# Gated delta stage: state update ahead of norm and key products' turn, first state products in other banks, dense copy of the block decay

## The reference, cut to what matters

```
def step(S, inp):                      # per head, S is 64 x 64
    qt, kt, vt, at, bt = inp
    err = jnp.einsum('bhij,bhj->bhi', S, kt) - vt
    S = at[..., None] * S - bt[..., None, None] * (err[..., None] * kt[:, :, None, :])
    o = jnp.einsum('bhij,bhj->bhi', S, qt)
    return (S, o)
...
o = (o - mu) / jnp.sqrt(var + EPS) * ln_w + ln_b
g = jax.nn.sigmoid(x @ Wg.T).reshape(Bb, Tt, H, DV)
o = (o * g).reshape(Bb, Tt, H * DV)
return o @ Wo.T
```

## Time and profile before

| | us |
|---|---|
| median of 3 runs | 3102.03 (3100.22 to 3104.4) |
| the profiled execution's own time | 3108.88 |
| its span | 3107.1 |
| PE busy | 2466.5 (79%) |
| PEld busy | 1716.8 (55%) |
| DVE busy | 2238.8 (72%) |
| ACT busy | 1270.0 (41%) |
| POOL busy | 272.3 (9%) |
| mean granted clock of TensorE | 0.860 of full speed |

### The profile page before, as it was taken

How to read it: one execution, slowest core, us unless ns; L and a number is a source line. 1 busy time by engine, 2 the same in 40 slices (tenths; PEclk the granted TensorE clock), 3 DMA queues, 4 the chain that set the end, 5 groups by cost and what they waited for, 6 DMA issues and landing times. The chain is left out here.

```text
span 3107.1 us, 64860 instructions
## 1 busy us (share of the span) xinstructions
PE 2466.5 (79%) x25297; PEld 1716.8 (55%) x25349; DVE 2238.8 (72%) x4089; ACT 1270.0 (41%) x2846; POOL 272.3 (9%) x281
## 2 busy tenths in 40 slices
PE   6877788887777777878956999999767756778776
PEld 5777777776777777763323666666322221222375
DVE  6999999999999999971033777777256656665555
ACT  3333333333333333323224777776411132556333
POOL 0000000000000000000031010100022311110342
PEclk9788878788888778879987999999978877999788
DMA  4111101111111101102018999995000001110521
GB/s 170 29 30 30 30 21 24 29 30 29 30 29 30 30 17 28 29 4 62 0 34 226 240 231 247 231 240 135 34 0 0 0 33 50 41 41 17 156 68 57
DMA packets 204444, 214.39 MB, mean 69 GB/s; under 512 B 31126, under 2 KB 190246, under 8 KB 198790
## 3 DMA queue, kind: packets, MB, share of 16 engines
q1 hardware_dynamic: 201769, 205.37, 25.5%
q0 software_dynamic: 2400, 4.94, 0.5%
HBM read 135.30 MB, written 74.70 MB: 68 GB/s over the span
## 5 line engine op out<-in xcount | busy, mean ns | idle before, releaser
L1284 DVE TENSOR_REDUCE ra_top<-ps 128x1 f32<-128x512 f32 x256 | 161.5, 684 | 96.5 <-PE ps L1088 90.7
L2552 DVE TENSOR_REDUCE dl_ZO<-dl_XP 128x64 f32<-128x128 f32 (+6 forms) x448 | 219.6, 490 | 15.4
L2226 PE MATMUL ps<-dl_kqN,dl_ST 64*64 64x32 f32 x4096 | 201.2, 274 | 18.2 <-DVE dl_ST L2575 18.2
L2226 PEld LDWEIGHTS ps<-dl_kqN,dl_ST 64*64 64x64 f32 x4096 | 198.7, 201 | 20.7 <-issue 20.7
L2548 DVE TENSOR_TENSOR dl_XP<-dl_ZO,dl_G 128x64 f32<-128x64 f32 (+6 forms) x448 | 194.6, 434 | 15.4
L1938 DVE TENSOR_TENSOR ps<-ps,da_window 128x192 f32<-128x192 f32 (+1 forms) x256 | 101.3, 396 | 122.2 <-PE ps L1667 117.9
L1205 ACT ACTIVATE ra_PT<-ps 128x512 f32<-128x512 f32 x256 | 136.8, 598 | 117.3 <-PE ps L1107 116.5
L1782 ACT ACTIVATE da_AB<-ps 128x384 f32<-128x384 f32 x256 | 124.5, 490 | 147.0 <-PE ps L1644 143.3
L1941 DVE TENSOR_REDUCE da_top<-ps 128x1 f32<-128x512 f32 x256 | 177.1, 692 | 8.8
L1792 ACT ACTIVATE da_E<-ps,da_top 128x512 f32<-128x512 f32 x256 | 176.0, 688 | 17.4 <-DVE da_top L1941 17.0
L1674 PE MATMUL ps<-ident,da_E 128*128 128x128 f32 x1024 | 169.1, 288 | 1.3 <-ACT da_E L1792 1.2
(11 more groups left out here) (401 smaller groups left out, 5706.1 us busy)
## 6 DMA issues: line engine op xcount, KB each, us to landing
da_bands<-da_AB SPq DMA_DIRECT2D x128, 384.0 KB, 3.8
dl_Abc<-dl_ends SPq DMA_DIRECT2D x64, 512.0 KB, 6.2
da_window<-da_bands SPq DMA_DIRECT2D x128, 192.0 KB, 4.4
da_across<-da_bands SPq DMA_DIRECT2D x128, 192.0 KB, 4.4
da_parts<-da_split SPq DMA_DIRECT2D x64, 96.0 KB, 3.3
rf_We<-in_rf_We SPq DMA_DIRECT2D x1, 4608.0 KB, 15.5
da_K<-da_parts SPq DMA_DIRECT2D x16, 256.0 KB
da_Q<-da_parts SPq DMA_DIRECT2D x16, 256.0 KB
```

The source lines that it names most:

```text
L1284: eng.tensor_reduce(top[:, m % 2, u:u + 1], ps[:, score_bank(UNITS * m + u), :], AXX, ALU.max, negate=True).then_inc(s["maxima"], 1)
L2226: mm = eng.matmul(start_ps[rows, pair, :], ST[rows, pair, :], kqN[rows, pair, e * CH:(e + 1) * CH, :].rearrange("p t k -> p (t k)"), start ...
L2552: link(eng.tensor_reduce(ZO[:, to:to + 1 + (2 * I - 1) * CH:CH].rearrange("p (k i) -> p k i", k=2), XP[:, :, :, SB - 1 - t:], AXX, ALU.add))
```

## The change: what it does

1. `first_ps`, banks 6 and 7, takes the starts for first halves (`starts_ps[0]`); those for second halves stay in banks 2 and 3. Since the updates 0 and 1 are read from banks 6 and 7, the starts of a first half wait for at least two state adds. The gate products, which also write banks 6 and 7, wait until the starts have been turned.
2. VectorE's `end` no longer holds `gate_keys` or `norm`. In their place ahead of the state adds stand the two turns of `prepare` (`turn_values`). `norm` comes after `prepare`, `gate_keys` after the state adds of the second half.
3. On TensorE the starts come ahead of the later products in the second half.
4. ScalarE copies the block decay, `F[:, e, :, 0, SB]`, into a dense tile `half` as the first instruction of its `middle`; VectorE's L2511 reads `half` and waits for the copy.

```diff
+        half = c.sb("dl_half", [P, 2, I], ctx)
...
+        first_ps = ps[:, 6:8, :].rearrange("p k (n x) -> p (k n) x", x=XC)
+        starts_ps = (first_ps, start_ps)
...
-                        mm = eng.matmul(start_ps[rows, pair, :], ST[rows, pair, :],
+                        mm = eng.matmul(starts_ps[e][rows, pair, :], ST[rows, pair, :],
...
                 def next_start(r):
-                    eng.wait_ge(s["state"], j4 + r + 1)
+                    eng.wait_ge(s["state"], j4 + max(r + 1, 2 * e))
...
+                for r in range(GR):
+                    next_start(r)
                 if e == 1:
                     eng.wait_ge(s["gt"], 2 * n + 3)
                     eng.sem_inc(c.past, 1)
                     later_products(n + 1)
-                for r in range(GR):
-                    next_start(r)
...
                 mm.then_inc(s["centred"], 1)
+                eng.wait_ge(s["begun"], BEGUN * (2 * n + 2) + 1)
                 for m in range(M):
...
             def middle(n, e):      # ScalarE
+                eng.wait_ge(s["transposed"], 3 * (2 * n + e + 1))
+                eng.activation(half[:, e, :], F[:, e, :, 0, SB], ACT.Copy).then_inc(s["halves"], 1)
                 eng.wait_ge(s["t"], 6 * n + 3 * e + 1)
                 eng.activation(WT[:, :, :], lists_ps, ACT.Copy).then_inc(s["wc"], 1)
...
-            def prepare(m, e):
-                at = 2 * m + e + 1
+            def turn_values(m, e):
                 span = slice(e * CH, (e + 1) * CH)
                 eng.wait_ge(s["evac"], m * PROJ + AV)
                 eng.transpose(aT[...], aN[...]).then_inc(s["transposed"], 1)
                 eng.transpose(bv[...], vN[...]).then_inc(s["transposed"], 1)
+
+            def prepare(m, e):
+                at = 2 * m + e + 1
...
-                eng.transpose(Y[:, :, :], start_ps.rearrange("p n x -> p x n")).then_inc(s["begun"], 1)
+                eng.transpose(Y[:, :, :], starts_ps[e].rearrange("p n x -> p x n")).then_inc(s["begun"], 1)
...
                 rest = Y[:, CH:, :]    # VectorE, middle
-                eng.tensor_tensor(rest, rest, F[:, e, :, 0, SB].unsqueeze(1).to_broadcast([P, CH, I]), ALU.mult).then_inc(s["begun"], 1)
+                eng.wait_ge(s["halves"], j + 1)
+                eng.tensor_tensor(rest, rest, half[:, e, :].unsqueeze(1).to_broadcast([P, CH, I]), ALU.mult).then_inc(s["begun"], 1)
...
             def end(n, e, first):
...
-                if e == 1:
-                    gate_keys(n + 1)
-                if e == 0 and not first:
-                    norm(n - 1)
+                turn_values(n + 1, e)
                 eng.wait_ge(s["decayed"], j + 1)
...
             def one_pass(n, first):
...
                 end(n, 0, first)
                 prepare(n + 1, 0)
+                if not first:
+                    norm(n - 1)
                 begin(n, 1)
...
                 end(n, 1, first)
+                gate_keys(n + 1)
                 if not first:
                     residual(n - 1)
                 prepare(n + 1, 1)
```

More of the change, by code:

```diff
@@ L2055, in delta_attention @@
              "gate", "var", "log", "scaled", "normed", "wo", "wo_copied", "transposed", "prefix", "prep", "whole",
-             "abc", "begun")
+             "abc", "begun", "halves")
     s = {n: c.nc.alloc_semaphore(name="dl_" + n) for n in names}
@@ L2617, in _ @@
             eng.wait_ge(s["beta"], 2)
-            prepare(0, 0)
-            prepare(0, 1)
+            for e in range(2):
+                turn_values(0, e)
+                prepare(0, e)
             empty_state()
```

## The result

The changed kernel takes 3150.8 us (median of 4 runs, 3143.9 to 3155.2) against 3101.4 us (4 runs): a ratio of 1.0159, 95% interval [1.0144, 1.0175]. That is +49 us, slower, as forecast, but beyond the +29 of the forecast and 4 us outside the range. The profiled execution took 3149.5 us (span 3147.7), 40.6 us more than the profiled one of before.

The account below looks back on a forecast made before the run. VectorE, busy 1166 of 1238 us, was taken to bound the stage. Terms 51.8 + 1.2 + 2.8 + 4.8 - 14.3 - 2.7 - 14.2 = +29.4 us on 3102.0 gave 3131 us, range 3096 to 3147.

Parts of the forecast that it names:

- The mechanism: Second halves: starts at low clock, later products last, so the path through TensorE and ScalarE makes L2511 wait, 51.8 us.
- first rival: Second-half starts: the clock stays as mixed as before, 30.7 us for 51.8, total 3110 us; chance 0.16.
- the idle time at the loop's end: TensorE idle between its last products and the key turn: 2.76 us in the low-clock path sum of 29.53 us.
- fourth rival: Path to L2511 grows by slower key turn, mean products or longer gap: 4.9 us at 14 boundaries, 3148 us; chance 0.11.
- The rest of the path: From L2544: starts begin 6.13 us, starts with later products 8.76, key turn to gates 11.63, copy 0.25; L2511 waits 3.7.
- The base: Time the sum is added to: median 3102.0 us of the runs shown; the profiled execution took 3108.9.
- Dense decay: VectorE's L2511 with a dense operand takes 665 ns instead of 1109, saving 14.2 us.
- First halves: VectorE's new order brings Y to 13.03 us after L2544, from 13.20: 0.17 each, saving 2.7 us.
- Second halves' middle: The copy stands behind output copy L2403, so L2511 waits: 0.3 us in each of 16, 4.8 us.
- Pass 0: Boundary after pass 0, with no idle time at the loop's entry: L2511 waits 1.2 us.
- The end of the stage: The last `centre` waits for ScalarE's four copies behind the later products: 2.8 us more.
- Rival 2: Second boundaries: the clock holds through all of them, making the kernel faster; chance 0.08.

Follow-up runs that it names:

- The run with the hint: The changed kernel with TensorE's loop telling its closing branch ahead, so the code at the loop's head can be fetched early: 3101.4 us, ratio 0.9999.
- the second half's part alone: The kernel before with starts ahead of later products, in banks 6 and 7, and `gate_keys` behind the adds, in second halves only: 3138.9 us, ratio 1.0125.
- The run with the spread held back: The changed kernel with the decay's spreading DMAs of second halves held until the next pass's keys are turned: 3136.2 us, ratio 1.0115.
- The second profile: The kernel before, unchanged, profiled once more: 3100.8 us, ratio 1.0002; the profiled execution took 3102.1 us.
- the run of that part alone: The kernel before with only the first half's order, turns ahead of the state adds and norm behind `prepare`: 3098.7 us, ratio 0.9981.
- the best version: The kernel before with the first half's order and the dense copy issued half a pass early, second halves as before: 3070.9 us, ratio 0.9906.

## Why the prediction was right or wrong

**The mechanism** was right in the main: the starts of second halves run at a granted clock of 0.50, wholly in four of the loop's 15 and in part in the others; the path through the loop's end and the gates comes late; the multiply waits for the copy behind it; dense copy and first halves gain little against that. The run with the hint takes the idle piece of the path away and the loss with it; the second half's part alone brings most of the loss. That the clock falls because the dense later products leave the gap behind the updates, as the forecast and its first rival have it, was my reading and was not tried by itself. In the seven profiled versions that have them last, all second starts of the loop took 5.7 to 7.0 us; in the seven that have them in the gap, 5 to 15 of 15 took 3.9. But banks, the place of the later products and VectorE's order changed together.

**The step that failed is a term of the sum:** the idle time at the loop's end, put at 2.76 us from one row of before for all 14 boundaries. It measured 53.3 / 14 = 3.81. In ten passes it was 2.9 to 3.4 us and in four, which had run their starts wholly at a granted clock of 0.50, 5.2 to 5.5. The prediction had this in its fourth rival ("as code and the decay's DMAs are fetched together"), with 3148 us the nearest of all its figures, and gave it 0.11. The run with the spread held back shows that it was this: 13.0 us of idle went, and the kernel gained 15. In the kernel before the DMAs that spread the decay (`Abc`) were issued some 0.6 us ahead of TensorE's end where a second half ran slow and some 3 us behind it where it ran fast; in the four long cases it was 1.1 to 1.4 us ahead (last section). So the change moved the two against each other by less than a microsecond, and that was enough.

Of the missing 20 us, 8.8 lie in the base (below) and 11.2 in the sum. The idle time alone was 14.7 us too small (53.3 - 14 x 2.76), and the other terms together 3.5 too large.

**The rest of the path** came out near: the multiply's waits (62.8) and the starts' (2.3) at the 14 boundaries sum to 65.0 us, 4.6 each where I had 3.7. Besides the idle time, key turn to gates took 12.45 us in the boundary shown, not 11.63, as the gate products ran partly at the low clock (3.07 us at a mean of 0.62, for 1.95); the starts with the later products took 8.23 us, not 8.76, as the clock fell while they ran (mean 0.56 over the starts); the copy cost 0.06 behind the gates and not 0.25, since its 0.23 us lie mostly under the last gate's.

**The base.** The sum was made on a profiled execution 7.5 us above the median of before, and I carried the difference over unchanged. The second profile shows that it lay in starts at a granted clock of 0.50, 4.6 us of it in second halves (8 slow against 5), where the changed kernel has this loss in every pass. Against the first profiled execution the change cost 40.6 us, against the second 47.4, on medians 49.4.

**Smaller terms.** Dense decay: 14.2 forecast, 13.4 measured. First halves: a saving of 0.17 a half forecast, 0.2 in the run of that part alone; the updates' end holds the adds, as written (13 waits of at most 0.3 us). Second halves' middle: 4.8 forecast, about 3 measured. Pass 0: 1.2 forecast, 1.14 measured. The end of the stage (2.8 forecast) can't be told apart from what varies behind it.

**The clock.** In the boundary shown the gap ahead of the starts was 2.0 us, and the clock fell in the first microsecond of the starts, which began at 379.62:

```profile
379.60:380.10 0.50, 0.48 (x17) 1.00 0.00 0
...
380.60:381.10 0.50, 0.50 (x14) 0.50 0.00 0
```

Rival 2, to which the prediction gave 0.08, was a clock that holds through all second boundaries. In none of the loop's 15 did it hold in the changed kernel: their starts took 5.83 to 7.04 us, where 3.92 is the time at 1.00. What makes the clock fall or hold is not shown by these runs.

## What to carry to other kernels

An engine that is idle beside the bounding one is free only as long as its path is not the last to arrive (here 41.4 us of idle cost nothing that can be told before the change, and 53.3 us cost about 49 after it): before moving work to the end of a loop body, follow that path through the branch to its first reader on the bounding engine. Don't carry the idle time at a loop's end over as a constant: here it was 2.9 to 3.4 us in ten passes and 5.2 to 5.5 in the four where the decay's DMAs had been issued earliest. Try a branch hint before building on it (here it gave 49 us where the path was late and nothing that can be told where it was not). And where the clock varies between executions, as here with 8 and 5 slow second halves in two profiles of one kernel, take the base from several profiles.

## What the runs showed of the hardware that was not expected

The idle time at TensorE's loop end, 53.3 us in 14 cases, vanished with a hint of the closing branch. I take it for the fetch of the loop's head, since the DMA view has a packet of instructions there that moves with the hint. In each of the 14 idle times of the changed kernel it has one packet on the queue that it calls instruction (q8; it does not name the engine), and the key turn starts 2.6 to 3.2 us after that packet starts. In the ten cases of about 3 us the packet starts 0.2 to 0.4 us after TensorE's end; there the spread's DMAs had been issued 0.2 to 0.9 us ahead of that end. In the four cases of 5.2 to 5.5 us they had been issued 1.1 to 1.4 us ahead, their transfers came first, and the packet starts only 2.0 to 2.4 us after the end. With the spread held back it starts within 0.6 us in all 14; with the hint it starts 3.1 to 3.5 us ahead of the key turn, and the idle time is gone. Queues of the DMA view (packets, MB, share) after pass 2, where TensorE ends at 300.77, first from there to 303.00, without a packet of q8, then from 303.00 to 303.50:

```profile
q1 hardware_dynamic: 68, 0.54, 105.5%
...
q8 instruction: 1, 0.02, 16.8%
```

After pass 3, where it ends at 387.85, the view to 388.30 has the packet already:

```profile
q8 instruction: 1, 0.02, 19.3%
```

For the idle time after pass 2 the stretches (us, TensorE busy, clock, DMA share, GB/s) show TensorE's end, the transfers and its return:

```profile
300.50:301.00 0.50, 0.27 (x8) 0.50 1.01 197
...
305.00:305.50 0.50, 0.00 (x0) 0.50 0.59 115
305.50:306.00 0.50, 0.00 (x0) 0.50 0.08 16
306.00:306.50 0.50, 0.30 (x2) 0.50 0.04 16
```

And small shifts of a dependent engine went with another clock: in the best version, with 0.4 us less in VectorE's middle and the first half's order, the number of second halves with slow starts was one of 16, where the two profiles of the kernel before had 8 and 5. What in these shifts decides the clock is not shown.
